# First two groups of the first stage reordered on all engines: shift, BC split, third statistics, weights one group later, products ahead of the next transposes

## What is computed

```python
xn = _layernorm(x, axis=-1)                     # x: 4 x 2048 x 512
# recurrence over the sequence, per channel, then a 512x512 product
h = h * A + x_t ;  s = einsum('sbd,do->bso', hs, BC)
# each token goes to the one of 8 experts with the highest score
scores = einsum('bsh,eh->bse', xn, gate_w) ; chosen = argmax(scores)
g = silu(xn + expert_w[chosen] @ xn)
out = x + s * g
```

## Time and profile before

| | us |
|---|---|
| timed runs | 529.09, 529.57, 530.28 |
| median | 529.57 |
| profiled execution, whole | 528.31 |
| its span, first to last record | 526.6 |
| PE busy in the span | 498.6 |
| DVE, POOL, ACT busy | 415.2, 317.9, 260.3 |

### The profile page before, as it was taken

How to read it: one execution, slowest core, us unless ns; L and a number is a source line. 1 busy time by engine, 2 the same in 40 slices (tenths; PEclk the granted TensorE clock), 3 DMA queues, 4 the chain that set the end, 5 groups by cost and what they waited for, 6 DMA issues and landing times. The chain is left out here.

```text
span 526.6 us, 10784 instructions
## 1 busy us (share of the span) xinstructions
PE 498.6 (95%) x2776; PEld 391.8 (74%) x2777; DVE 415.2 (79%) x1068; ACT 260.3 (49%) x500; POOL 317.9 (60%) x358
## 2 busy tenths in 40 slices
PE   6699999999999999999987999999999999999993
PEld 6466776777777777777776888888888888887882
DVE  5979899899989998999732677777777777777773
ACT  4556676677677667767720333333333333333330
POOL 3535756766766676666644366666766666656652
PEclk9989999999999999999988999999999999999998
DMA  8995777887877787787346467776867777757720
GB/s 235 383 344 159 249 218 237 254 229 249 263 238 235 240 260 217 249 266 239 114 124 203 138 222 240 230 250 217 268 224 228 227 234 214 228 193 249 228 80 10
DMA packets 65411, 116.98 MB, mean 222 GB/s; under 512 B 8842, under 2 KB 26250, under 8 KB 65300
## 3 DMA queue, kind: packets, MB, share of 16 engines
q1 hardware_dynamic: 47328, 64.59, 39.2%
q0 software_dynamic: 18048, 52.02, 31.3%
HBM read 66.27 MB, written 57.48 MB: 235 GB/s over the span
## 5 line engine op out<-in xcount | busy, mean ns | idle before, releaser
L983 PE MATMUL ps_s<-w_hi,split 128*128 x284 | 118.8, 418 | 0.1
L596 ACT ACTIVATE ps_s<-ps_s 128x512 f32<-128x512 f32 x71 | 41.3, 582 | 154.5 <-issue 94.5
L470 POOL DMA_INDIRECT out_dram<-work x71 | 73.7, 1038 | 71.8 <-issue 45.3
L984 PE MATMUL ps_s<-w_lo,split 128*128 x284 | 112.9, 398 | 0.0
L985 PE MATMUL ps_s<-w_hi,split 128*128 x284 | 112.8, 397 | 0.0
L902 PE MATMUL ps_s<-bc_hi,split 128*128 128x512 f32 x256 | 105.3, 411 | 0.0
L903 PE MATMUL ps_s<-bc_lo,split 128*128 128x512 f32 x256 | 102.4, 400 | 0.0
L460 POOL DMA_INDIRECT work<-token_rows,work x71 | 72.6, 1023 | 31.1 <-issue 24.4
L394 POOL TENSOR_TENSOR split<-work,split 128x1024 fp32r<-128x1024 f32 x32 | 76.2, 2380 | 10.1 <-ACT split L524 9.9
L412 POOL DMA_INDIRECT slot_table<-token_id,slot_id x64 | 63.0, 985 | 26.1 <-issue 20.9
L638 DVE TENSOR_TENSOR_SCAN work<-a_col,work,ps_xt 128x256 f32<-128x256 f32 x112 | 74.3, 725 | 0.2
(11 more groups left out here) (103 smaller groups left out, 734.1 us busy)
## 6 DMA issues: line engine op xcount, KB each, us to landing
token_rows<-work SPq DMA_DIRECT2D x31, 528.0 KB, 3.1
work<-in_L_attn_inputs_dram SPq DMA_DIRECT2D x31, 512.0 KB
token_rows<-work SPq DMA_DIRECT2D x29, 512.0 KB
work<-in_L_ffn_expert_w_dram SPq DMA_DIRECT2D x128, 64.0 KB
slot_table<-w_lo SPq DMA_DIRECT2D x1, 4160.0 KB, 17.8
token_rows<-in_L_attn_inputs_dram SPq DMA_DIRECT2D x3, 512.0 KB
work<-token_rows,work POOLq DMA_INDIRECT x71
out_dram<-work POOLq DMA_INDIRECT x71
```

What stands on the lines that cost most here:

```text
L470: nc.gpsimd.indirect_dma_start(out=out_flat, out_offset=bass.IndirectOffsetOnAxis(ap=slot_tok[:, n:n + 1], axis=0), in_=o_sb[:, u], in_off ...
L983: nc.tensor.matmul(z_ps[v], hi, wh, start=(k == 0), stop=False)
L984: nc.tensor.matmul(z_ps[v], hi, wl, start=False, stop=False)
```

## The change

A constant `SIDE = 2` is added. BC is split in halves: ACT and DVE take two row blocks, POOL the other two. On DVE `deviation` of group 1 moves behind `scan` of group 0, statistics of group 2 move ahead of `scan` of group 1, and `turn_w(c)` stands in group c, where `turn_w(c + 1)` stood; `block_low` and ACT's `block_high` follow one group later, and on POOL so does `add_identity`. ACT takes `copy_parts` of group 0 ahead of `high_part`, and `root` of group 2 ahead of the copies of group 1. PE does half of the high products of groups 0 and 1 ahead of the next group's transposes.

```diff
--- before.py
+++ after.py
@@ -58,6 +58,7 @@
     FILL = 640
     PLANNED = -(-TILES // 16) * 16
     LATE = 1
+    SIDE = 2
     Q = 32
     LAST = (GROUPS - 1) % 2
     EMPTY = TOKENS
@@ -416,16 +417,15 @@
 
 
             pool.wait_ge(bc_loaded, 16)
-            nc.gpsimd.tensor_copy(bc_hi[:, CH - 1], bc_raw[:, CH - 1]).then_inc(bc_last_hi, 1)
+            nc.gpsimd.tensor_copy(bc_hi[:, SIDE:], bc_raw[:, SIDE:]).then_inc(bc_last_hi, 1)
             pool.wait_ge(bc_last_hi, 1)
-            nc.gpsimd.tensor_tensor(bc_lo[:, CH - 1], bc_raw[:, CH - 1], bc_hi[:, CH - 1],
+            nc.gpsimd.tensor_tensor(bc_lo[:, SIDE:], bc_raw[:, SIDE:], bc_hi[:, SIDE:],
                                     ALU.subtract).then_inc(bc_lo_done, 1)
-            add_identity(0, 0)
+            low_part(0, 0)
             pool.wait_ge(bc_lo_done, 2)
             nc.gpsimd.memset(s_out[:, :, :, O + 2:], 0.0).then_inc(pad_ready, 1)
-            low_part(0, 0)
             next_ids(0, 0)
-            add_identity(0, 1)
+            add_identity(0, 0)
 
             def group(it, c, left=2):
                 count(it, c)
@@ -433,8 +433,8 @@
                     low_part(it, c + 1)
                     next_ids(it, c + 1)
                 scatter_ids(it, c)
-                if left >= 2:
-                    add_identity(it, c + 2)
+                if left >= 1:
+                    add_identity(it, c + 1)
 
             for c in range(GROUPS):
                 group(0, c, left=GROUPS - 1 - c)
@@ -548,15 +548,16 @@
             copy_head(0, 0)
 
             act.wait_ge(bc_loaded, 16)
-            nc.scalar.copy(bc_hi[:, :CH - 1], bc_raw[:, :CH - 1]).then_inc(bc_hi_done, 1)
+            nc.scalar.copy(bc_hi[:, :SIDE], bc_raw[:, :SIDE]).then_inc(bc_hi_done, 1)
+            copy_parts(0, 0)
             high_part(0, 0)
-            copy_parts(0, 0)
             normalise(0, 1, 0)
             normalise(0, 1, 1)
+            root(0, 2)
 
             def group(it, c, left=3, start=False):
-                if left >= LATE:
-                    block_high(it, c)
+                if not start:
+                    block_high(0, c - 1)
                 if left >= 1:
                     copy_tail(it, c + 1)
                     copy_head(it, c + 1)
@@ -566,7 +567,6 @@
                     high_part(it, c + 1)
                 if start:
                     copy_parts(0, 1)
-                    root(0, 2)
                 if left >= 2:
                     normalise(it, c + 2, 0)
                 if left >= 1 and not start:
@@ -730,29 +730,30 @@
                 statistics(0, c, start=(c == 0))
                 dve.wait_ge(stats_done, c + 1)
                 variance(0, c)
-                for step in range(5):
-                    deviation(0, c, step)
+                if c == 0:
+                    for step in range(5):
+                        deviation(0, c, step)
             dve.wait_ge(const_ready, 14)
             dve.wait_ge(a_loaded, 16)
             scan(0, 0)
+            for step in range(5):
+                deviation(0, 1, step)
             dve.wait_ge(bc_hi_done, 1)
-            nc.vector.tensor_tensor(bc_lo[:, :CH - 1], bc_raw[:, :CH - 1], bc_hi[:, :CH - 1],
+            nc.vector.tensor_tensor(bc_lo[:, :SIDE], bc_raw[:, :SIDE], bc_hi[:, :SIDE],
                                     ALU.subtract).then_inc(bc_lo_done, 1)
-            turn_w(0)
             route(0, 0, False, behind=False)
+            statistics(0, 2)
+            dve.wait_ge(stats_done, 3)
+            variance(0, 2)
 
             def group(it, c, left=3, start=False):
                 if left >= 1:
                     scan(it, c + 1)
-                if start:
-                    statistics(0, 2)
-                    dve.wait_ge(stats_done, 3)
-                    variance(0, 2)
                 if left == 0:
                     place(it, c, 0)
                     place(it, c, 1)
-                if left >= LATE:
-                    block_low(it, c)
+                if not start:
+                    block_low(0, c - 1)
                 if start:
                     for step in range(5):
                         deviation(0, 2, step)
@@ -762,8 +763,8 @@
                     wait(dve, mv_taken, U * it + c)
                     dve.sem_inc(mv_free, 1)
                     variance(it, c + 3)
+                turn_w(c)
                 if left >= 1:
-                    turn_w(c + 1)
                     route(it, c + 1, left >= 3)
 
             for c in range(GROUPS):
@@ -926,22 +927,27 @@
             pe.wait_ge(gate_ready, 1)
             score_parts(0, 0)
             scores(0, 0)
-            turn_x(0, 1)
             pe.wait_ge(bc_lo_done, 2)
 
-            def group(it, c, turned=False):
-                if not turned:
+            def group(it, c, first=False):
+                if first:
+                    product_hi(it, c, 0)
                     turn_x(it, c + 1)
-                product_hi(it, c, 0)
-                product_hi(it, c, 1)
-                score_parts(it, c + 1)
-                product_lo(it, c, 0)
+                    product_hi(it, c, 1)
+                    product_lo(it, c, 0)
+                    score_parts(it, c + 1)
+                else:
+                    turn_x(it, c + 1)
+                    product_hi(it, c, 0)
+                    product_hi(it, c, 1)
+                    score_parts(it, c + 1)
+                    product_lo(it, c, 0)
                 product_lo(it, c, 1)
                 scores(it, c + 1)
                 ranks(it, c)
 
             for c in range(4):
-                group(0, c, turned=(c == 0))
+                group(0, c, first=(c < 2))
             with pe.Fori(1, GROUPS // 4 - 1) as it:
                 for c in range(4):
                     group(it, c)
```

## The result

| | us |
|---|---|
| before, median of 6 runs | 529.29 (526.62 to 530.28) |
| changed kernel, median of 6 runs | 524.21 (522.29 to 525.29) |
| ratio, after to before | 0.9904, 95% interval 0.9878 to 0.993 |
| profiled execution of after, whole and span | 522.29, 520.6 |

So the change makes the kernel 5.1 us faster, 0.96% (0.7 to 1.2%). A second set of runs of both kernels gave a ratio of 0.988 (0.9831 to 0.9928).

A forecast was written before the change was run, and what follows sets the result against it. The prediction took PE, busy nine tenths and more in nearly all slices, as the bound. Its terms 0 - 0.2 - 2.0 + 0 + 0.4 gave -1.8 us, from 529.57 to 527.8 us, range 524.8 to 529.6.

The forecast's parts named there:

- Start: Up to group 3's transposes at 37.04 us: no net gain, 0 us (0.3 either way).
- The barrier: Store of group 3's raw x, landing at 35.5 us, holds `normalise(3, 0)` and takes back the start's whole gain.
- The lock's working: In BC, two-input DVE and POOL instructions exclude each other; first high product between 15.6 and 18.0 us, 18.0 taken.
- Group 2: 37.04 to 46.00 us: a 1.28 us stall goes, slow matmuls may cost 1.1; -0.2 us (-1.3 to +0.3).
- Groups 3 to 7: 46.00 to 86.69 us: POOL's wait for weights goes, `low_part` starts earlier, stalls shrink; -2.0 us (-2.4 to -0.7).
- Groups 8 to 30: After 86.69 us, 22 groups at 7.67 us each: nothing changes, 0 us (-0.5 to +0.3).
- The hand-over: Between the stages: the last `add_identity` now stands between POOL's last scatters, delaying the gather; +0.4 us (0 to +0.5).
- (a): Rival: the start's gain arrives because group 3's store lands earlier or does not hold PE; 523.7 us, chance 0.12.
- (b): Rival: the long groups between 46 and 87 us stay long, -0.3 instead of -2.0; 529.5 us, chance 0.19.
- (c): Rival: slower, L651 meets `low_part` in every group, 27 groups pay 0.14 us, +3.8; 531.6 us, chance 0.10.

The follow-up runs named there:

- e1: The kernel before with only the rotation of the weights (one group later), the start as it was; 523.78 us, ratio 0.9879.
- r_before_a: The kernel before, unchanged, measured and traced a second time; 529.54 us, ratio 0.9994.
- e2: The changed kernel with the weights back where they stood before, so only the reordered start stays; 527.84 us, ratio 0.9973.
- e9: The changed kernel with one small unused two-input POOL instruction ahead of `low_part` in groups 9 to 30; 526.63 us, ratio 0.9949.
- r_after: The changed kernel, unchanged, measured and traced a second time; 524.23 us, ratio 0.988.
- e3: The changed kernel with BC split three to one as before (`SIDE = 3`); 524.08 us, ratio 0.99.
- e4: The changed kernel with SP's three copies of x moved from the start to the last groups of the first stage; 521.08 us, ratio 0.9835.

## Why the prediction was wrong, point by point

**Start, 0: the mechanism right, its margin of 0.3 too narrow.** Group 3 came 1.3 us earlier than in the one trace shown, and 0.4 earlier by the means. The barrier was read rightly off one row: `normalise(3, 0)` waits for the store in all three traces of before and both of after, and is released between 33.81 and 35.56. But a landing that moves by 1.75 us was given 0.3 us either way, and the sign that rested on it failed: not 35.5 with a wait of 3 us and more, but 34.26 with 0.37 and 34.11 with 2.45. The lock's working was half right. The first product came at 17.72 in one trace and at 15.79 in another, the two ends that had been given (18.0 and 15.6). "PE reaches `scores(2)` at 32 to 33" held in the second (it was idle from 32.1), and was 34.3 in the first, where the eight slow matmuls were paid at 17.7; the sum that gave 32 had none in it. The sentence that DVE can wait for POOL only once was wrong there: L651 and L663 both stood, 2.10 and 2.26 us.

**Group 2 (37.04 to 46.00), -0.2 (-1.3 to +0.3): right, and both its ends came.** It took 7.58 in one trace (-1.4), 9.06 in the other (+0.1 against the same row, +0.3 against the mean of before). The stall of L651 is gone in both; whether the low clock falls here decides between the two.

**Groups 3 to 7, -2.0 (-2.4 to -0.7): mechanism right, size 0.45 to 0.8 us short.** Measured 40.69 to 38.24, -2.45, and -2.8 by the means; so the transposes of group 9 stood at 81.57 and not at the 84.0 to 85.0 of the forecast's sign. The working had 38.3 as the floor, and that is what came (38.24, 38.04). I took less than the floor because two of the groups had no long L651. But the lateness of one group is handed on: all of it goes with the stalls, as e1 shows (38.22 with nothing but the weights moved).

**Groups 8 to 30, 0 (-0.5 to +0.3): the step that failed.** It measured -1.5 against the same trace, and -3.1 by the means. The working said that 7.67 was 0.06 above the undisturbed 7.61 and that "most of it comes with each fourth group, where PE's loop turns". The rows for the other reading were there. L651 at 110.29 took 0.29 us, not 0.15, and I used it for the rival that gets slower, not for the sum. One view would have sized it: the group of L651 between 90 and 250 us has a mean of 0.291 us in 21 instructions, so 2.9 us of stall, where the changed kernel has 0.159. So the place was read rightly and the cause was not: each fourth group was long by stalls of L651, its own or those handed on to it. In the changed kernel, where L651 is at most 0.25 us and PE's loop turns at the same place, up to 0.24 us of it is left. In the end the same cause, POOL late for the weights, works in all groups: long stalls in the first ones, short ones later, and now and then a long one again (r_before_a).

**The hand-over, +0.4: right in its term.** From the transposes of group 31 to the issue of the last scatter: 13.05, 13.07 and 13.08 us in the traces of before, 13.48 and 13.49 after. The gather behind it moves by some 0.65 us on its own, since the wait for the scatters' landing is 1.80 or 2.45 us in either kernel.

**The base.** The sum was made against the one trace shown, with 526.6 us of span the shortest of three. The mean saving is larger against the others, because what the change takes away is also what varies: 168.70, 170.10 and 172.00 before, 167.22 and 167.20 after.

**The rivals.** (a) did not come: on top of the weights no gain of the start can be seen, though a time near its 523.7 came, for another reason. That is a time that fits the wrong story. Its sign, group 3 well before 37, came too (35.75) and told nothing, since before itself has it at 35.30 and 35.88; only e1 and e2 tell them apart. (b) fell, and (c) too: L651 is at most 0.25 us in all groups after group 2. But its mechanism was real in the kernel before, with the other sign. Its price was also summed wrongly: 3.8 "in place of the 2.0 saved" is -1.8 + 2.0 + 3.8 = +4.0, not +2.0.

**The range** left out a value 0.6 us below it. Its lower end was made of the sum's own -2.8 and a part of rival (a). With the measured -1.5 of the same trace for groups 8 to 30 the sum is -3.3, and with the mean's -3.1 it is -4.9, against 5.1 measured; that it comes so near is in part luck, since the start and groups 3 to 7 were off too and the part to the end scatters by more.

The Trainium skill's page SBUF — State Buffer, section Who interferes with whom, says that issue order decides which of the two is blocked. The traces agree: POOL's L395 was 0.09 us ahead of DVE's L663 in one run and DVE's L742 was 0.05 us ahead of POOL's L395 in the other, and each time the later one stood (2.26 against 0.16 us; 3.44 against 2.34 us).

## What to carry to other kernels

Before a steady loop is written down as undisturbed, take the mean of the short instructions in it and compare it with their shortest: 0.291 against 0.15 us was 2.9 us of stall in 21 groups that looked regular. A short stall is not free if it comes in each round: in e9 0.25 us a round put DVE some 0.15 us further behind each time, until PE waited. So a distance that is long only now and then doesn't by itself point to the engine that turns its loop there. And where a step's price hangs on when a DMA lands, trace the kernel before more than once: what varies between its traces may be just what the change takes away.

## What the runs showed of the hardware

- The access that DVE and POOL share goes to either by a few hundredths of a microsecond (POOL 0.09 us ahead in one trace, DVE 0.05 in the other), and the same program goes both ways: its first product was at 17.72 and at 15.79 us, 1.9 apart.
- It works in both directions: POOL's `low_part` of 2.34 us took 3.44 while DVE's instruction of 1.22 us ran.
- The wait of the gather for the last scatter's landing takes one of two values, 1.77 to 1.81 or 2.43 to 2.47 us, over all kernels in which the gather waited for it. What sets it was not tried.
- Stretches in which PE had stood 3.13 us (r_after) and 4.12 us (after) were followed by a granted clock of 0.50, that is 1.2 GHz. In e3, which stood 4.22, the clock was 0.50 from 36 to 38 us as well, and group 3 to 4 took 8.77 us. In the first trace of after the 1.06 us ahead of 35.38 were followed by a clock of 1.00 and 7.58 us. The length of the stand alone doesn't tell: e4 stood 1.23 us ahead of 15.58 and was granted 0.50 from 16 to 19 us, while r_after stood 1.80 us ahead of 15.79 and kept 1.00.
